# Linear attention with a mixture of experts: projections three chunks ahead of attention in place of two, and eight buffers for v in place of four

## What is computed

```python
q, k = elu(x @ Wq.T) + 1.0, elu(x @ Wk.T) + 1.0
v = x @ Wv.T
kv_cumsum = cumsum(einsum('blhd,blhe->blhde', k, v), axis=1)
k_cumsum = cumsum(k, axis=1)
out = einsum('blhd,blhde->blhe', q, kv_cumsum)
out = out / clip(einsum('blhd,blhd->blh', q, k_cumsum), 1e-06)
x = layernorm(x + out @ Wo.T)
# router: top 2 of 8 experts by softmax of the RMS-normalised x
# expert e: (gelu(x @ g0[e].T) * (x @ g1[e].T)) @ linear_w[e]
x = layernorm(x + sum_of_the_two_weighted_experts)
```

## Time and profile before

| | |
|---|---|
| median of 3 runs | 236.42 us (236.21 to 236.98) |
| the profiled execution | 237.81 us |
| its span, first to last instruction | 235.9 us |
| PE busy | 160.1 us, 68% |
| DVE busy | 152.2 us, 64% |
| POOL busy | 123.3 us, 52% |
| ACT busy | 92.1 us, 39% |
| chain that ended last, by engine | PE 29%, DVE 20%, issue 17%, POOL 14%, DMA 8%, ACT 7% |

### The profile page before, as it was taken

The page is one execution under the profiler, slowest core; times in us unless marked ns, Lnnn a source line. Parts: engine busy times, 40 slices in busy tenths (PEclk is TensorE's granted clock), DMA queues, the critical chain, the costliest instruction groups (busy, mean ns, idle before and its releaser), DMA issues.

```text
span 235.9 us, 3616 instructions
## 1 busy us (share of the span) xinstructions
PE 160.1 (68%) x780; PEld 115.4 (49%) x781; DVE 152.2 (64%) x485; ACT 92.1 (39%) x312; POOL 123.3 (52%) x110
## 2 busy tenths in 40 slices
PE   2887998495495872988414000999999999972560
PEld 0454654363363551665314000687888888851440
DVE  0569999768877688689544890365666666630761
ACT  3234465161153522045422100465656566630270
POOL 5683550913336676327157771055666666661760
PEclk9999999989589796599555555699999999998575
DMA  5749200000000001001001362212323233214732
GB/s 157 210 93 394 94 15 22 0 11 11 0 24 3 23 11 37 12 11 47 25 11 45 92 173 53 67 48 80 89 79 92 81 90 85 78 47 139 264 89 67
DMA packets 18624, 17.52 MB, mean 74 GB/s; under 512 B 2881, under 2 KB 16193, under 8 KB 18481
## 3 DMA queue, kind: packets, MB, share of 16 engines
q1 hardware_dynamic: 16304, 12.66, 18.7%
q0 software_dynamic: 2304, 4.69, 6.2%
HBM read 10.61 MB, written 6.73 MB: 74 GB/s over the span
## 4 chain that ended last, share of the span: by engine, by line
PE 29%; DVE 20%; issue 17%; POOL 14%; DMA 8%; ACT 7%; SPq 1%; POOLq 1%; DVEq 0%; ACTq 0%
DVE prod L942 7%; POOL zbuf L458 6%; POOL both L489 6%; PE bank L535 6%; PE bank L522 3%; PE bank L702 3%; DVE num L949 3%; ACT junk L773 2%; PE bank L691 2%; DMA zin<-zbuf 2%; DMA pl<-both 2%; PE bank L693 2%; PE bank L692 2%; DMA both<-yout,zin 2%; PE bank L730 2%
## 5 line engine op out<-in xcount | busy, mean ns | idle before, releaser
L489 POOL DMA_INDIRECT both<-yout,zin x39 | 37.4, 960 | 33.0 <-issue 17.8
L444 POOL TENSOR_TENSOR kv<-v,qk 128x1152 f32<-128x1152 f32 x16 | 34.9, 2178 | 25.0 <-DVE qk L916 24.9
L535 PE MATMUL bank<-kv,C 128*128 128x432 f32 (+1 forms) x96 | 39.6, 555 | 6.2 <-DVE prod L942 6.2
L458 POOL DMA_INDIRECT zbuf<-rows,slot x32 | 32.4, 1012 | 17.0 <-issue 8.6
L535 PEld LDWEIGHTS bank<-kv,C 128*128 128x128 f32 x96 | 19.7, 221 | 23.0 <-issue 15.0
L942 DVE TENSOR_TENSOR prod<-bank,qk 128x432 f32<-128x432 f32 (+1 forms) x48 | 24.5, 548 | 2.2 <-PE bank L535 2.2
L702 PE MATMUL bank<-w_l,actT 128*128 x156 | 24.6, 280 | 1.1 <-ACT actT L878 1.1
L702 PEld LDWEIGHTS bank<-w_l,actT 128*128 128x128 f32 x156 | 20.4, 190 | 8.6 <-issue 8.6
L682 PE MATMUL bank<-C,zin 128*128 128x128 f32 x39 | 11.3, 290 | 17.8 <-DMA zin<-zbuf 17.8
L1195 DVE COPY yout<-bank 128x128 f32<-128x128 f32 x39 | 11.4, 292 | 18.3 <-PE bank L702 18.3
L916 DVE SCALAR_TENSOR_TENSOR qk<-eqk,rqk 128x256 f32<-128x256 f32 x16 | 12.8, 799 | 14.8 <-ACT v L743 14.8
(11 more groups left out here) (140 smaller groups left out, 317.3 us busy)
## 6 DMA issues: line engine op xcount, KB each, us to landing
zin<-zbuf SPq DMA_DIRECT2D x39, 65.0 KB, 1.9
w_g<-in_gate_w SPq DMA_DIRECT2D x4, 512.0 KB, 6.1
pl<-both SPq DMA_DIRECT2D x8, 256.0 KB, 4.9
xTs<-in_xT SPq DMA_DIRECT2D x16, 64.0 KB, 2.1
w_l<-in_lin_w SPq DMA_DIRECT2D x1, 1024.0 KB, 9.3
out<-pl SPq DMA_DIRECT2D x8, 128.0 KB, 1.8
both<-yout,zin POOLq DMA_INDIRECT x39, 2.2
zbuf<-pads SPq DMA_DIRECT2D x8, 65.0 KB, 2.3
```

The costliest lines, as they stand in the source:

```text
L444: pool.tensor_tensor(kv[:, s, :].rearrange("p (h e d) -> p h e d", e=HE, d=HD), a, b, ALU.mult).then_inc(kv_done, 1)
L458: pool.indirect_dma_start(zbuf, bass.IndirectOffsetOnAxis(ap=slot[:, g, r, j:j + 1].bitcast(U32), axis=0), rows[:, GROUP * g + j, r, :], N ...
L489: pool.indirect_dma_start(both, bass.IndirectOffsetOnAxis(ap=zin[:, b, D + 1:D + 2].bitcast(U32), axis=0), yout[:, b, :], None).then_inc(p ...
L535: pe.matmul(pre_ps[b][:, 0:c1 - c0], const("tri"), kv[:, s, c0:c1], start=True, stop=True)\
```

## The change

PE and ACT do `project` and `inputs` of chunk m + 3 in step m, not m + 2, in all three places of each engine where it can stand. The common order `groups` starts one step earlier (m = -3). DVE's `features` and POOL's `outer` stay at m + 2. `v1` has 2 * `GROUP` = 8 buffers; its three users index it by n modulo 8, and L743 waits for the chunk eight before. The memset of ones at the start covers 1152 columns in place of 576. `qkv_ps` stays one bank, `eqk` and `rqk` stay two buffers, `qk` and `kv` four. In the changed kernel line numbers behind `groups` are lower by 2.

```diff
-        v1 = sb("v1", [P, GROUP, H * HE])
+        v1 = sb("v1", [P, 2 * GROUP, H * HE])
...
-            for m in range(-2, 2):
-                step(0, m, None)
-            for m in range(2, 6):
+            for m in range(-3, 6):
                 step(0, m, None)
...
-                a = v1[:, s, :].rearrange("p (h e) -> p h e", e=HE).unsqueeze(3).to_broadcast([P, H, HE, HD])
+                a = v1[:, n % (2 * GROUP), :].rearrange("p (h e) -> p h e", e=HE).unsqueeze(3).to_broadcast([P, H, HE, HD])
...
                 if route == 2:
                     if exists(g, m - 1):
                         prefix(g, m - 1)
-                    if exists(g, m + 2):
-                        project(g, m + 2)
+                    if exists(g, m + 3):
+                        project(g, m + 3)
...
-                if exists(g, m + 2) and not first:
-                    project(g, m + 2)
+                if exists(g, m + 3) and not first:
+                    project(g, m + 3)
                 if isinstance(g, int) and g == 0 and m == -1:
                     clear_state()
                 if exists(g, m - 1):
                     prefix(g, m - 1)
                 if first:
-                    project(g, m + 2)
+                    project(g, m + 3)
...
-                after(ac, state_done, n - GROUP + 1)
-                after(ac, kv_done, n - GROUP + 1)
-                ac.activation(v1[:, m % GROUP, :].rearrange("p (h e) -> p h e", e=HE)[:, :, 0:HD],
+                after(ac, state_done, n - 2 * GROUP + 1)
+                after(ac, kv_done, n - 2 * GROUP + 1)
+                ac.activation(v1[:, n % (2 * GROUP), :].rearrange("p (h e) -> p h e", e=HE)[:, :, 0:HD],
...
                 else:
-                    if exists(g, m + 2):
-                        inputs(g, m + 2)
+                    if exists(g, m + 3):
+                        inputs(g, m + 3)
```

More of the change, by code:

```diff
@@ L541, in state @@
                 pe.wait_ge(state_used, n + 1)
-                pe.matmul(state_ps, qk[:, s, D:2 * D], v1[:, s, :], start=False, stop=False,
+                pe.matmul(state_ps, qk[:, s, D:2 * D], v1[:, n % (2 * GROUP), :], start=False, stop=False,
                           skip_group_check=True).then_inc(state_done, 1)
```

## The result

| | before | after |
|---|---|---|
| median | 236.59 us (236.21 to 236.98, 4 runs) | 227.27 us (226.52 to 229.68, 4 runs) |
| ratio, with its 95% interval | | 0.962 (0.955 to 0.970) |
| profiled execution | 237.81 us | 227.32 us |
| its span | 235.9 us | 225.5 us |
| granted clock, mean of the span | 0.829 | 0.852 |

The change is worth 9.3 us in the medians and 10.5 us between the two profiled executions; predicted were 226.1 us, a gain of 10.3. The engines do the same work as before. What has gone is the wait that the prediction named. L914 (L916 before) and what it waited for, by line: busy times, idle before it, and who waited for it.

What follows compares the result with a forecast made beforehand. Bound: DVE's L916 waiting for ACT's L743, 14.8 us in ten waits. Terms 5.2 + 5.3 - 0.2 = 10.3 us off the median 236.42 gave 226.1 (227.5 profiled); range 223.8 to 229.2.

Steps and rivals of the forecast that it cites:

- Group 1: Chunks 9, 10 and 11: 2.53 + 1.69 + 0.99 = 5.21 us gained.
- the row in the tail: L1235, two SBUF inputs, took 0.16 inside L503, the same operation as L450; so L450 would not hold L916.
- The covers of 0.8 and 2.2: Group 1 slack before DVE would wait: 0.8 us for chunk 10's logits, 2.2 for chunk 11's ranks from PE.
- Chunk 12: Route 0 of group 2: the 1.40 wait goes, nothing gained; three products later L985 waits 1.6 for ACT's squares.
- Group 2: Chunks 13 to 15: 2.5 + 0.99 + 1.78 = 5.3 us gained, with chunk 14's L916 held by a kv.
- The start: Fourth and fifth projections stand before first prefix and first read-out: 0.2 us lost, first product near 15.16.
- The good end and the bad end of the prediction: At the start: all fits at full clock; at the low level the prefix takes 4.05, up to 2.2 us late.
- rival 1: Group 3: PE's idle shrinks, L535 may take 2.0 for 4.05 at full clock; 1.7 gained, 224.4; chance 0.15.
- (2): Group 1, chunk 9: L450 holds L916, then kv; group gives 1.69 + 0.99, in all 7.8, 228.6; chance 0.13.
- (3): Group 1: L1030 loses to chunk 9's kv also, till 47.4; 2.2 less, 228.3; chance 0.05.
- (4): Everywhere ACT's squares, zT and logits end last, nothing gained, 236.4; chance 0.03.
- (5): Start on the low clock costs 2.2 us; slower if routing steps return less, 237.6 with 1 returned; chance 0.04.

Runs made afterwards that it cites:

- Experiment 9: Kernel before, with POOL's kv behind the mean and ahead of the power in route 0, behind the shift in route 1: 231.47 us, ratio 0.972.
- experiment 12: Changed kernel, kv behind mean (route 0), shift (route 1) and second product (route 3), route 1's scatters behind kv: 219.71 us, ratio 0.928.
- experiment 3: Changed kernel, with POOL's kv ahead of the power in route 0 and waiting for the shift in route 1: 225.68 us, ratio 0.950.
- Experiment 6: Changed kernel, with projections three chunks ahead only up to group 1 and two ahead from group 2 on: 231.02 us, ratio 0.973.
- 10: Changed kernel, kv behind mean (route 0) and shift (route 1), route 0's projection and ACT's reads behind prefix and copies: 223.37 us, ratio 0.938.
- experiment 2: Kernel before, with only v1 changed to eight buffers: 237.74 us, ratio 1.001.
- 11: 10, with route 3's kv waiting for the step's second product and route 1's scatters behind kv: 220.34 us, ratio 0.926.

## Why the prediction was right

**The bound.** L916's wait for L743 was the right row to start from, and the question put to it, what is late next, was answered place by place. Experiment 9 shows that the waits are the gain itself, 4.11 for 4.03 in group 1.

**Group 1: 5.21 predicted, 5.39 measured.** L914 of chunk 9 ran for 0.41 inside the power L448 (42.08 to 43.74): not held, as the row in the tail had it. L1028 was held, by the first kv alone: it ended at 45.90, in the middle of the pair of 4.30. It gained 47.77 - 45.90 = 1.87, and with the 0.68 that all is later at chunk 8, 2.55 against 2.53. L982 was held as foreseen, 1.84. The covers of 0.8 and 2.2 held: DVE waits for neither logits nor ranks.

**Chunk 12: nothing, for another reason.** The prediction had DVE idle 1.6 at L985, waiting for ACT's squares. DVE idled 1.27 at the products L940, waiting for PE's prefix, and 0.21 at L983. The squares wait for PE in the end as well, so the sum is the same, -0.11; the step that failed is "three products later": the prefix itself is late, because PE starts its chain of state, projection and prefix only at the read of the ranks, and does most of it at the low clock (granted 0.50 from 60.0 to 61.5 and 0.58 to 63.3):

```profile
60.19 1.49 PE L520 MATMUL bank<-w_qkv,xTs 128*128 128x384 f32 x2
...
61.68 2.76 PE L533 MATMUL bank<-kv,C 128*128 128x432 f32 x6
```

**Group 2: 5.3 predicted, 5.36 measured.** L1028 was held and ended at 71.72 against 77.70, 5.98 less the 4.60 that L983 had gained by then, 1.38 (1.36 predicted). L914 of chunk 14 met the kv of 74.22, took 2.04 and ended at 76.70, before at 83.80: 7.10 in all, less the 4.60 of L983, so 2.50 in this group (2.5). L982 free, 0.16 (0.17). This was the part with the most room for error, and it came out because kv's own times had been moved along with DVE's.

**The start: -0.2 predicted, -0.68 measured.** The first product stood at 15.20 (15.16 before), as said. The prediction also had L956 follow its sum without idle, and that failed: PE's first read-out ran up to 18.48 and L956 came right behind it, 0.45 after L925, which started at 18.07, in place of 0.21.

```profile
17.97 0.51 PE L544 MATMUL bank<-state_m,qT 128*128 128x144 f32 x2 [0.83 <-ACT qT L749]
```
```profile
18.52 0.32 DVE L956 TENSOR_TENSOR bank<-bank,num 128x144 f32<-128x144 f32 x1
```

That is 0.24 of the 0.68; another 0.32 came at the next products, for which DVE waits for PE's second prefix. The term is a spread more than a number: PE passes from the low clock to the full one at some point of the first prefix, and that point differs. PE's first prefix, its six multiplies, in experiment 12 and in experiment 3, which have the same order of PE there:

```profile
13.01 2.72 PE L540 MATMUL bank<-kv,C 128*128 128x432 f32 x6
```
```profile
13.00 4.05 PE L537 MATMUL bank<-kv,C 128*128 128x432 f32 x6
```

Chunk 8 came at 36.85 in the one and at 38.51 in the other, 0.1 and 1.8 behind before; after, with 3.17 for the same six, it came 0.7 behind. The good end and the bad end of the prediction (4.05, up to 2.2) both exist. But the old order has this spread as well. Experiment 6 starts in the new order and experiment 9 in the old one, and both had a first prefix of 3.83:

```profile
13.06 3.83 PE L539 MATMUL bank<-kv,C 128*128 128x432 f32 x6
```
```profile
10.43 3.83 PE L540 MATMUL bank<-kv,C 128*128 128x432 f32 x6
```

Chunk 8 came at 38.01 and 37.67, so the order costs 0.34 at a like clock. In all nine profiles in the new order chunk 8 goes with the length of that prefix (2.72 to 4.05 us, 36.85 to 38.51), and in the four in the old one too (2.89 to 3.83, 36.71 to 37.67). Of the 0.68, about half is then the order, near the 0.2 of the prediction, and the rest that the prefix took 3.17 in this profile and 2.89 in that of before. This is worked out from one profile of each kernel, not from a run made for it.

**Group 3 and rival 1.** PE's idle ahead of L540 fell from 2.62 to 0.85, and the prefix behind it still took 3.83 at the low clock (4.05 before). Rival 1 gave 1.7 for this; 0.2 came, from 84.42 to L983 at 93.07 (94.38 to 103.26 before: 8.65 against 8.88). The other 0.5 that group 3 gave are in its later rows. What rival 1 hoped for exists, but is not tied to the change: the same prefix took 2.10 in experiment 12 and 3.86 in 10, and 2.48 in experiment 9, where the projections are two ahead and PE had idled 2.60 before it.

**The rivals.** (2) and (3) are put away by the two rows above, L914 at 42.22 and L1028's end. (4) by the missing waits, (5) by the size of the start. The Trainium skill's rule ("SBUF — State Buffer", section "Who interferes with whom") would have had L448 hold L914. The trace does not agree: L914 took 0.41 and 0.42 inside it, in both groups. For kv the rule agrees with L1028 (2.13) and L914 (2.04), which have two inputs in SBUF. L982 (1.84) and, in experiment 3, L1011 (1.33) have one, and were held too.

**The sum.** 10.67 up to the last ranks for 10.3. In the medians the gain was 9.3, and the median is 1.2 above the forecast. Why the medians gave 9.3 where the marks give 10.67 stays open: no run isolates it. The part behind the last ranks, which varied by 4 us between the profiles, is wide enough for it. In experiment 2, which runs as before does (last ranks at 130.82 in place of 130.43), that part took 104.1 in place of 105.5.

## What to carry to other kernels

Where one engine waits for another that reads its input "only then", take each wait apart: subtract it, and walk on until the next instruction that needs something; then move the neighbour's long instructions by the same amount, because they decide whether a small instruction of four numbers costs 0.16 or 2.1 us. An instruction held in this way is worth moving the other engine for: here one kv moved ahead of a power and two waits of POOL on semaphores that DVE sets anyway were worth 5.9 us in the medians, 4.1 of it the two holds by the profile, against the 9.3 of the change. And a difference of half a microsecond that one profile shows in a stretch at a changing clock is no finding until a second kernel with the same edit shows it too.

## What was not expected of the hardware

- A RECIPROCAL of DVE with both ends in SBUF is not held by a kv: L964 of before ran at 80.13 for 0.25, its usual time, inside the kv of 78.83 to 81.02, where TENSOR_SCALAR and TENSOR_TENSOR of four numbers with their inputs in SBUF take up to 2.13.
- DVE, waiting since the start of one kv, gets in between two that POOL runs back to back: L1028 ended at 45.90 within the pair of 43.72 to 48.02, and the pair took 4.30, twice 2.15. Here one hold cost one kv, not both.
- The power of eight numbers on POOL (1.66 us) holds no two-input instruction of DVE that ran within it (0.41 and 0.42).
- With the same idle of PE ahead, 0.52, the granted clock stayed at the 2.4 GHz level in one profile (11) and fell to the 1.2 GHz level in the other (12); one group later, with the same order and the same 0.87 of idle, it was the other way round. The six executions of kernel 12 had mean granted clocks from 0.848 to 0.872 and took 221.8 to 218.1 us. What decides it stays open.
